# A second layer norm with its own statistics, placed three attention steps before the end, in a fused attention and expert kernel

## The reference

```python
x = x + xattn(layernorm(x), ctx, ctx, mask, Wq, bq, Wk, bk, Wv, bv, Wo, bo)
f = layernorm(x)
xa = f @ P_w.T
C1, C2, C3 = (top3_softmax(xa @ U.T) for U in (U1, U2, U3))   # [tokens, 12], 3 non-zero
h = gelu(sum_e C1[:, e] * (f @ W1[e].T))
y = sum_e C2[:, e] * (h @ W2[e].T) + C3 @ b2
x = x + y
```

## Time and profile before

| | |
|---|---|
| median of 3 runs | 412.53 us (411.24 to 412.81) |
| the profiled execution | 412.67 us |
| its span | 410.9 us |
| TensorE busy | 392.6 us, 96% |
| VectorE busy | 341.1 us, 83% |
| ScalarE busy | 115.8 us, 28% |
| GpSimd busy | 110.9 us, 27% |
| mean granted clock of TensorE | 0.988 of 2.4 GHz |

### The profile page before, as it was taken

How to read it: one execution, slowest core, us unless ns; L and a number is a source line. 1 busy time by engine, 2 the same in 40 slices (tenths; PEclk the granted TensorE clock), 3 DMA queues, 4 the chain that set the end, 5 groups by cost and what they waited for, 6 DMA issues and landing times.

```text
span 410.9 us, 7824 instructions
## 1 busy us (share of the span) xinstructions
PE 392.6 (96%) x2132; PEld 333.4 (81%) x2132; DVE 341.1 (83%) x1036; ACT 115.8 (28%) x263; POOL 110.9 (27%) x165
## 2 busy tenths in 40 slices
PE   4699999999989999999999999999999999999996
PEld 4479889898878788888888888888888888888884
DVE  3788898898895889798898978989788898888875
ACT  3467888888921211010101101011010101101000
POOL 5462647466540211202022020211202022020200
PEclk9889999999989999999999999999999999999999
DMA  7900131222000000000000000000000000000000
GB/s 228 331 0 3 52 102 54 99 87 66 2 0 2 1 2 14 13 0 13 0 13 0 13 13 0 13 0 13 13 0 13 0 13 3 10 13 0 14 0 26
DMA packets 8612, 12.71 MB, mean 31 GB/s; under 512 B 1076, under 2 KB 5016, under 8 KB 8472
## 3 DMA queue, kind: packets, MB, share of 16 engines
q1 hardware_dynamic: 8040, 12.44, 9.2%
q10 hardware_dynamic: 560, 0.13, 0.1%
HBM read 10.47 MB, written 2.10 MB: 31 GB/s over the span
## 4 chain that ended last, share of the span: by engine, by line
PE 87%; DVE 4%; issue 3%; ACT 3%; POOL 1%; DMA 1%; ACTq 0%; POOLq 0%; DVEq 0%
PE banks L920 67%; PE banks L997 4%; PE banks L987 3%; PE banks L962 2%; PE banks L972 2%; PE banks L975 2%; PE banks L977 2%; PE banks L1035 1%; DVE q_hl L625 1%; DMA bk_sb<-in_bk_dram 1%; PE banks L1043 1%; PE banks L1025 1%; ACT w_h L534 1%; PE banks L1008 1%; POOL w_l L366 1%
## 5 line engine op out<-in xcount | busy, mean ns | idle before, releaser
L815 DVE SCALAR_TENSOR_TENSOR s_d<-banks,c_cur,s_d 128x256 f32<-128x256 f32 x165 | 72.6, 479 | 25.2 <-PE banks L920 22.2
L920 PE MATMUL banks<-w_h,xf_h 128*128 128x512 f32 x204 | 81.8, 401 | 0.0
L920 PE MATMUL banks<-w_l,xf_h 128*128 128x512 f32 x204 | 80.3, 394 | 0.0
L920 PE MATMUL banks<-w_h,xf_l 128*128 128x512 f32 x204 | 80.2, 393 | 0.0
L406 POOL TENSOR_TENSOR top_e<-euler,top_d 128x9 f32<-128x9 f32 x16 | 28.9, 1806 | 183.2 <-DVE top_d L765 183.2
L920 PE MATMUL banks<-w_h,h_h 128*128 128x512 f32 x180 | 73.0, 406 | 0.0
L920 PE MATMUL banks<-w_l,h_h 128*128 128x512 f32 x180 | 70.5, 392 | 0.0
L920 PE MATMUL banks<-w_h,h_l 128*128 128x512 f32 x180 | 70.1, 390 | 0.0
L815 DVE SCALAR_TENSOR_TENSOR sum<-banks,c_new,sum 128x256 f32<-128x256 f32 x160 | 66.2, 478 | 3.1 <-PE banks L920 3.1
L561 ACT ACTIVATE h_h<-banks 128x256 fp32r<-128x256 f32 x15 | 5.8, 384 | 153.8 <-PE banks L1043 153.8
L920 PEld LDWEIGHTS banks<-w_l,xf_h 128*128 128x128 f32 x204 | 38.7, 190 | 8.4
(11 more groups left out here) (126 smaller groups left out, 624.3 us busy)
## 6 DMA issues: line engine op xcount, KB each, us to landing
stage<-in_w_t_dram SPq DMA_DIRECT2D x12, 512.0 KB, 3.6
out_dram<-x_all SPq DMA_DIRECT2D x16, 128.0 KB, 1.9
x_all<-in_x_dram SPq DMA_DIRECT2D x1, 1024.0 KB, 7.3
x_all<-in_x_dram SPq DMA_DIRECT2D x1, 768.0 KB, 7.9
mask_all<-in_mask_dram SPq DMA_DIRECT2D x2, 256.0 KB, 5.0
x_all<-in_x_dram SPq DMA_DIRECT2D x2, 128.0 KB, 3.8
wk_sb<-in_wk_t_dram SPq DMA_DIRECT2D x1, 256.0 KB, 3.7
wq_sb<-in_wq_t_dram SPq DMA_DIRECT2D x1, 256.0 KB, 4.5
```

Of the source, the lines that this page charges most:

```text
L815: dve.scalar_tensor_tensor(out=sums[e % 2][:, :], in0=product, scalar=weights[:, e:e + 1], in1=sums[e % 2][:, :], op0=ALU.mult, op1=ALU.ad ...
L920: ins = pe.matmul(dst, a(c), b(c), start=(i == 0), stop=(i == len(terms) - 1))
```

## The change

1. The second norm has `bn2`, `mean_var2`, `var_eps2` and `rstd2` of its own. They are allocated behind all other buffers, which stay where they were.
2. `stats2(0)` stands ahead of VectorE's `attention(T - 4)`, `normalise2(0)` directly behind it. GpSimd's `inverse_deviation2(0)` moves from the last weight chunk to the one before. TensorE's and ScalarE's programs keep the place of tile 0.
3. `xf_h` and `xf_l` are made from `ps_t` in PSUM and no longer from `xf_t`. ScalarE no longer waits between the two copies, nor for `xf_lo` of the tile before. The instructions that overwrite `ps_t` next (the transposes of `xf` of tile 1 and of `h`) wait for `xf_lo` in place of `xf_copied`.
4. `xf_low(0)` stands ahead of `stats2(1)`, not behind it.

```diff
+        bn2 = sb("bn2", [P, 6])
+        mean_var2 = sb("mean_var2", [P, 2])
+        var_eps2 = sb("var_eps2", [P, 1])
+        rstd2 = sb("rstd2", [P, 1])
...
+            def inverse_deviation2(t):
+                pool.wait_ge(stats2_ready, t + 1)
+                pool.tensor_tensor(var_eps2[:, :], mean_var2[:, 1:2], eps[:, :], ALU.add).then_inc(var2_ready, 1)
+                pool.wait_ge(var2_ready, t + 1)
+                pool.tensor_tensor(rstd2[:, :], var_eps2[:, :], minus_half[:, :], ALU.pow).then_inc(rstd2_ready, 1)
...
                     add_output_bias(T - 1)
-                    inverse_deviation(0, stats2_ready, var2_ready, rstd2_ready)
+                if n == CHUNKS - 2:
+                    inverse_deviation2(0)
                 split_weights(n, n % RING)
...
                 if later(t, 1):
                     act.wait_ge(z_done, t)
-                    act.wait_ge(xf_lo, t)
                 nc.scalar.activation(xf_t[:, :, :], ps_t, ACT.Copy).then_inc(xf_copied, 1)
-                act.wait_ge(xf_copied, t + 1)
-                nc.scalar.activation(xf_h[:, :, :], xf_t[:, :, :], ACT.Copy).then_inc(xf_hi, 1)
+                nc.scalar.activation(xf_h[:, :, :], ps_t, ACT.Copy).then_inc(xf_hi, 1)
...
+            def stats2(t):
+                statistics(t, bn2, mean_var2, bn2_done, stats2_ready)
...
             def normalise2(t):
-                dve.wait_ge(xft_done, t)
-                normalise(t, x_all, xf, rstd2_ready, xf_ready)
+                if later(t, 1):
+                    dve.wait_ge(xft_done, t)
+                dve.wait_ge(rstd2_ready, t + 1)
+                dve.tensor_scalar(xf[:, :], x_all[:, t, :], mean_var2[:, 0:1], rstd2[:, 0:1],
+                                  ALU.subtract, ALU.mult).then_inc(xf_ready, 1)
...
+            stats2(0)
             attention(T - 4)
-            statistics(0, x_all, bn2_done, stats2_ready)
+            normalise2(0)
 
             def xf_low(t):
+                dve.wait_ge(xf_copied, t + 1)
                 dve.wait_ge(xf_hi, t + 1)
-                dve.tensor_tensor(xf_l[:, :, :], xf_t[:, :, :], xf_h[:, :, :].bitcast(F32), ALU.subtract).then_inc(xf_lo, 1)
+                dve.tensor_tensor(xf_l[:, :, :], ps_t, xf_h[:, :, :].bitcast(F32), ALU.subtract).then_inc(xf_lo, 1)
...
             a_low(T - 4)
-            normalise(0, x_all, xf, rstd2_ready, xf_ready)
             q_low(T - 1)
             divide_by_sum(T - 3)
             add_attention(T - 4)
-            statistics(1, x_all, bn2_done, stats2_ready)
             xf_low(0)
+            stats2(1)
...
                 pe.wait_ge(xf_ready, t + 1)
                 if later(t, 2):
                     pe.wait_ge(h_lo, t - 1)
+                elif t == 1:
+                    pe.wait_ge(xf_lo, 1)
                 else:
-                    pe.wait_ge(xf_copied if t else xt_copied, 1 if t else T)
+                    pe.wait_ge(xt_copied, T)
...
                 n = min(t + 2, T) if isinstance(t, int) else t + 2
-                pe.wait_ge(xf_copied, n)
+                pe.wait_ge(xf_lo, n)
```

More of the change, by code:

```diff
@@ L350, in _, with inverse_deviation @@
             pool.wait_ge(consts_set, 16)
[L352 to L357, removed]
+            def inverse_deviation(t):
+                pool.wait_ge(stats_ready, t + 1)
+                pool.tensor_tensor(var_eps[:, :], mean_var[:, 1:2], eps[:, :], ALU.add).then_inc(var_ready, 1)
+                pool.wait_ge(var_ready, t + 1)
+                pool.tensor_tensor(rstd[:, :], var_eps[:, :], minus_half[:, :], ALU.pow).then_inc(rstd_ready, 1)
+            def inverse_deviation2(t):
[3 more added lines that the diff above has]
+                pool.tensor_tensor(rstd2[:, :], var_eps2[:, :], minus_half[:, :], ALU.pow).then_inc(rstd2_ready, 1)
             def add_output_bias(t):
@@ L369, in attention @@
             def attention(t):
-                inverse_deviation(t, stats_ready, var_ready, rstd_ready)
+                inverse_deviation(t)
                 add_output_bias(t - 1)
-            inverse_deviation(0, stats_ready, var_ready, rstd_ready)
-            inverse_deviation(1, stats_ready, var_ready, rstd_ready)
+            inverse_deviation(0)
+            inverse_deviation(1)
             pool.wait_ge(setup_dve, 5)
             place_low_keys(pool, 0, kbd_set)
-            inverse_deviation(2, stats_ready, var_ready, rstd_ready)
+            inverse_deviation(2)
             pool.wait_ge(bo_in, 16)
@@ L425, in _ @@
             exponentials(0)
-            inverse_deviation(1, stats2_ready, var2_ready, rstd2_ready)
+            inverse_deviation2(1)
             exponentials(1)
@@ L429, in _ @@
             with pool.Fori(2, T) as t:
-                inverse_deviation(t, stats2_ready, var2_ready, rstd2_ready)
+                inverse_deviation2(t)
                 exponentials(t)
@@ L592, in _, with statistics @@
         def _(dve):
-            def statistics(t, src, done, ready):
-                dve.bn_stats(bn[:, :], src[:, t, :]).then_inc(done, 1)
+            def statistics(t, parts, dst, done, ready):
+                dve.bn_stats(parts[:, :], x_all[:, t, :]).then_inc(done, 1)
                 dve.wait_ge(done, t + 1)
                 dve.memset(waited[:, :], 0.0)
[L598 to L603, removed]
+                dve.bn_aggr(dst[:, :], parts[:, :]).then_inc(ready, 1)
             def stats1(t):
-                statistics(t, x_all, bn_done, stats_ready)
+                statistics(t, bn, mean_var, bn_done, stats_ready)
+            def stats2(t):
+                statistics(t, bn2, mean_var2, bn2_done, stats2_ready)
             def normalise1(t):
@@ L610, in normalise1 @@
                     dve.wait_ge(xt_done, t)
-                normalise(t, x_all, xn, rstd_ready, xn_ready)
+                dve.wait_ge(rstd_ready, t + 1)
+                dve.tensor_scalar(xn[:, :], x_all[:, t, :], mean_var[:, 0:1], rstd[:, 0:1],
+                                  ALU.subtract, ALU.mult).then_inc(xn_ready, 1)
             def normalise2(t):
-                dve.wait_ge(xft_done, t)
-                normalise(t, x_all, xf, rstd2_ready, xf_ready)
+                if later(t, 1):
[3 more added lines that the diff above has]
+                                  ALU.subtract, ALU.mult).then_inc(xf_ready, 1)
             def q_low(t):
@@ L884, in experts @@
                 if ahead:
-                    statistics(t + 2, x_all, bn2_done, stats2_ready)
+                    stats2(t + 2)
                 layer1_pairs(t + 1, range(0, 3))
```

## The result

The changed kernel takes 408.63 us as median of 6 runs (408.29 to 409.91). The kernel before, beside it, takes 411.91 us (6 runs, 411.18 to 412.88). The ratio is 0.9933, with a 95% interval of 0.9914 to 0.9952: 0.67% or 3.3 us faster.

A forecast was written before the change was run, and what follows sets the result against it. It took the handover from attention to experts as the bound, with TensorE full in the loop. −1.59, −0.1, +0.69 and +0.1 summed to −0.9 us: 411.6 us from the median 412.53, range 409.7 to 412.9.

The forecast's parts named there:

- xf_l and xf_h from PSUM: Tile 0 at the handover from attention to experts: xf_l no longer held by GpSimd, −1.59 us; xf_h sooner, −0.1 us.
- The statistics behind xf_l: VectorE at the handover: tile 1's statistics, moved behind xf_l, now stand on the chain, +0.69 us.
- The delay from the early statistics: Tile 0's statistics ahead of attention(12) on VectorE delay everything behind by 0.1 us, bounds 0 and 0.35.
- normalise2(0) as cover and not gain: Ahead of tile 14's maxima: tile 15's scores start up to 0.41 us sooner, only lengthening TensorE's later a_l wait.
- The clock: Behind output_project(13)'s wait, 119.0 to 122.4 us at 1.2 GHz: costs about 1.6 us, kept in the forecast.
- rival 1: Clock stays at 2.4 GHz through the handover in the median run: 2.5 us gained, 410.0 us; chance 0.33.
- The level to subtract from: The forecast's starting time: 412.53 us, the median of the runs before, from which the gain was taken.
- Rival 2: Tile 1's statistics (bn) are held inside GpSimd's w_l instead of xf_l: 412.9 us, slower than before; chance 0.08.
- Rivals 3 and 4: 3: second clock fall at 125 us, 414.5 us, chance 0.04. 4: only 0.55 us gained, 412.0; shares forecast's 0.55.

The follow-up runs named there:

- psum_only: The kernel before with only xf_h and xf_l made from PSUM, all else as before; 408.20 us beside 411.31 (ratio 0.9939).
- w_l_later: The kernel before, with GpSimd's last w_l subtraction waiting until xf_l of tile 0 is there; 408.12 us beside 411.45 (ratio 0.9909).
- stats_first: The changed kernel with the statistics of tile 1 put back ahead of xf_low(0); 408.09 us beside 411.31 (ratio 0.9930).
- fill_before: The kernel before with four extra matmuls, results unread, in TensorE's 1.56 us wait ahead of output_project(13); 409.72 us beside 411.31 (ratio 0.9974).
- longer_wait: The changed kernel with two extra bn_stats on VectorE ahead of a_l of tile 13; 410.63 us beside 411.45 (ratio 0.9969).
- norm_only: The changed kernel with xf_h and xf_l made from xf_t in SBUF as before; 411.81 us beside 411.31 (ratio 1.0016).

## Why the prediction was wrong

- **xf_l and xf_h from PSUM: right, in size too.** Forecast −1.59 and −0.1; `psum_only` measures 13.02 − 11.33 = 1.69 us: xf_l takes 1.58 us less and begins 0.11 sooner against the scores of tile 14. xf_h took 0.378 us as median of 16 in the changed kernel, straight behind xf_t. `w_l_later` shows the overlap with GpSimd as the cause; that had only been argued.
- **The statistics behind xf_l: right, a little too dear.** Forecast +0.69, measured +0.53 by `stats_first`. With the 1.69 us above, that is the whole of the 1.16 us.
- **The delay from the early statistics: nil.** Forecast +0.1, up to 0.35. The distance from the scores of tile 13 to those of tile 14 is 6.15 us before and after. Against the scores of tile 14 the maxima of tile 13 were 0.2 us late, and xn of tile 15 began 0.15 us late, took 0.49 us in place of 0.64 and so ended where it had. The sum at the projection is −1.16 us against −0.9.
- **normalise2(0) as cover and not gain: right.** TensorE's wait of 0.41 us on q_low went, and the same time stands before a_l. Only with ScalarE's copies ahead does the early norm shorten the handover, by 0.58 us. What the title names is thus not what made the kernel faster.
- **The clock: the step that failed.** The prediction's sum has no term for the clock: it took the stretch at 1.2 GHz behind the projection as staying in the median run, with odds "somewhat below even" for rival 1, in which it goes. It went: the wait in front fell from 1.56 to 0.99 us, and the profile shows 1.00 behind it. The price was right: 1.6 us forecast, 1.5 between the profiles of before and after. The argument against rival 1 was the fall near 27 us behind a wait of only 0.46 us. It did not carry over: the profile of the changed kernel has the same wait there, of 0.47 us, and no fall, so that fall was one of the execution. That the clock behind the projection depends on how much TensorE stands idle in front is now shown from both sides, by `fill_before` and `longer_wait`.
- **The level to subtract from: the second half of the miss.** Even rival 1 gave 410.0. The sum went out from 412.53, the middle of three runs, which belongs to the highest of the three groups of before (near 409.9, 411.2 and 412.7 us; the middle one is the largest). So does the profile of before, at 412.67: besides the handover it paid 1.3 us near 27 us, a fall which the earlier trace rows showed and the prediction used only as evidence on the odds. The profile of `fill_before`, at 409.70 with the same handover, has neither fall, and lies where the lowest group does; the middle group itself was not profiled, and that it pays for one fall is inferred from its level. From the middle group, 411.2 − 1.16 − 1.6 gives 408.4, where four of the six runs after lie (408.29 to 408.66). The other two, at 409.8 and 409.9, are 1.3 us above, the price of a fall near 27 us; those two were not profiled, so that place is inferred.
- **Rival 2: refuted.** bn ran inside w_l in 0.42 us. **Rivals 3 and 4:** nothing of either was seen in the profile of the changed kernel.

So of the 3.3 us between the medians 1.16 us are steps and 1.5 to 1.6 us are the clock at the handover. The remaining 0.5 to 0.6 us are put down to how often the clock fell elsewhere in the two sets of six (three of the six runs of before lie in the highest group); that is argued from the groups, not measured.

## What to carry to other kernels

When one instruction of a form takes several times its median, look at what GpSimd does at that moment, and whether both operands lie in SBUF: here an operand in PSUM, or a later start of GpSimd's work, was enough, and rearranging the stage around it may be needless. An instruction moved behind such a stall to make room can land on the chain itself; leave short independent work in the gap that is there. When one experiment changes two things, as `norm_only` does, see which of them its loss belongs to. Where TensorE waits just before a dense stretch, price the clock behind it as a term of its own, and before subtracting from a median look whether the runs fall into groups, and in which the profiled one lies.

## What was not expected of the hardware

- The runs of one kernel lie in groups 1 to 1.6 us apart. The two stretches at 1.2 GHz that cost such a step in a profile lie near 27 us (1.3 us) and behind the projection (1.5 us). An earlier one, between 12.7 and 20 us, moved the scores of tile 14 by 0.3 us at most.
- Filling 1.56 us of waiting with four matmuls whose results nobody reads made the kernel 1.6 us faster.
- A plain f32 matmul of 256 columns ran as two instructions of some 0.25 us each (1.54 us over 6), so three of them took 1.5 us where 0.47 us of waiting were to be filled. The four matmuls of `fill_before`, whose operands are of type fp32r, ran as one instruction each (2136 matmuls on its page, 2132 before).
- VectorE's xn of tile 15 (one tensor input, both sides in SBUF) ends 0.14 to 0.16 us after GpSimd's x_all in all fourteen profiles, and takes 0.41 to 0.64 us, the longer the sooner it begins behind x_all's start: 0.64 us beside x_all in the earlier trace rows, where the same form without it takes 0.40 (xf above). No experiment moved x_all, so that x_all holds it is read from the times alone.
